# Larger expert blocks, rows scattered by slot and a combined last stage in a one-core decoder layer

## The chip, the core and the metric

The kernel runs on one core of one Trainium2 chip. The metric is the device time of one execution in microseconds; 5482.36 is the median of three runs of the kernel before (5481.67 to 5484.12). A core has a matrix engine (TensorE, PE), a vector engine (VectorE, DVE), a scalar engine (ScalarE, ACT), a programmable engine (GpSimd, POOL) that also issues indirect transfers, and a queue engine (SyncE, SP) that issues plain transfers. All transfers run on 16 shared DMA engines.

## The reference

One decoder layer on 16 sequences of 224 tokens with 512 features, 3584 tokens in all. It is a quantised self-attention, a cross-attention over 750 context rows, and a third block of attention across the 16 sequences followed by a mixture of experts. Only the last part and the norm behind it are touched:

```python
h1 = hidden_states + proj
ln2 = _layer_norm(h1, ln2_weight, ln2_bias)
probs = jax.nn.softmax(x @ router_weight, axis=-1)
top_p, top_i = jax.lax.top_k(probs, 2)          # 2 of 8 experts, shares normalised
cap = int(np.ceil(N * K / E * 1.25))            # 1120 slots for each expert
dst = jnp.where(within < cap, sorted_exp * cap + within, T)   # slot of each (token, choice)
padded_tokens = jnp.zeros((T, H)).at[dst].set(x[order // K], mode='drop')
fc1 = jax.nn.gelu(jnp.einsum('ech,ehf->ecf', xt, moe_w1))     # 512 -> 1024
fc2 = jnp.einsum('ecf,efh->ech', fc1, moe_w2)                 # 1024 -> 512
moe_out = jnp.zeros((N, H)).at[padded_tid].add(fc2 * padded_probs[:, None])
return h1 + moe_out
# and outside: x = _layernorm(x + ffn(x))
```

## The kernel before

The program is a row of stages. A stage is a `phase` (its semaphores, cleared by GpSimd when it ends) with one block in which each engine has its own instruction stream; the next stage starts when all engines have ended. Tokens stand in 28 tiles of 128 rows (`TT`), tile g of partition p being token 28p + g in the later stages.

Early in the program stands the stage `qm` (from line 422). TensorE computes all q, k and v products from rows and weights that are already in SBUF, and VectorE takes their largest magnitude. SP, ScalarE and GpSimd have nothing to do in it.

The end of the program is this:

- Stage `rt` (line 1792): the normalised rows `h1` are multiplied by the router's weights on TensorE; beside it SP stores `h1` to the DRAM table `l2_d` and zeros to `tid_d`. The residual `base` (x plus h1) stays in SBUF to the end of the program.
- Stage `sl` (line 1881): VectorE takes the two best experts of each token and gives each choice its slot; then GpSimd scatters token numbers by slot into `tid_d` with 56 indirect DMAs of 128 numbers (line 1889).
- Stage `tid` (line 1977): the token numbers are loaded, made float, turned on TensorE and copied back as integers, so that a column of them serves one tile.
- Stage `mo` (line 1994): the experts. `E` = 8 experts, each with `BLOCKS` = 5 blocks of `BT` = 2 tiles of `TS` = 112 slots. `loop4` runs three times over two experts in a hardware loop and then two experts written out. For each block GpSimd gathers the rows of the next block by token number (line 2052). TensorE multiplies with everything split into a high and a rest part, so each product is three matmuls (`three`, lines 2082 to 2084): first weights as stationary operand and 224 transposed token columns moving (8 groups f, two of which share a PSUM bank, 96 matmuls a block); then it transposes the next block's rows (line 2073, one bank for each tile, 8 transposes); then the second product, with gelu columns stationary (112) and 512 weight columns moving, 24 matmuls a tile. ScalarE does the gelu and the rounding to the high part (lines 2160, 2165), VectorE the rest part (line 2201), and both split the next block's transposed rows (lines 2151, 2194). The weights of the next expert are split beside it. SP loads weights (lines 2024, 2025) and stores the block's result rows to `y_d` (line 2037).
- Stage `cb` (line 2228): for each of 28 tiles GpSimd copies the slot numbers (line 2238) and gathers the two expert rows of each token (line 2242, 56 indirect DMAs of 256 KB), and VectorE adds them with their shares to `base` (lines 2257, 2259). Four tiles may be under way.
- Stage `nf` (`normalised`, line 254): VectorE takes the statistics of all tiles, ScalarE a square root, VectorE the inverse deviations and then the scaling.
- Stage `out` (line 2261): one store of 7168 KB.

TensorE, VectorE and ScalarE take their instructions in order; a waiting instruction holds up everything behind it on its engine.

## Time and profile before

| | |
|---|---|
| median of three runs | 5482.36 us |
| profiled execution | 5477.36 us |
| its span | 5475.4 us |
| PE busy | 3870.9 us (71%) |
| DVE busy | 2829.8 us (52%) |
| ACT busy | 1760.5 us (32%) |
| POOL busy | 654.2 us (12%) |
| moved by DMA | 266.11 MB |

Busy times are of the whole span, in which stages with different limits follow each other. The profile gives for each instruction its start, its duration, its shape and what ended the engine's idle time before it. `<-issue` stands for time in which the engine waited for nothing that the profile shows. The durations of a matmul overlap with the next one's; the distance of their starts is the pace. PEclk is the granted clock, 1.00 for 2.4 GHz and 0.50 for 1.2 GHz.

### The profile page before, as it was taken

How to read it: one execution, taken by the hardware profiler on the slowest of the kernel's cores; microseconds unless marked ns; L12 is line 12 of the kernel's file. 1: busy time of each engine (PE TensorE's matmuls, PEld its weight loads, DVE VectorE, ACT ScalarE, POOL GpSimd, SP SyncE). 2: the span in 40 equal slices, each digit the busy share in tenths (PEclk: the TensorE clock that was granted, in tenths of full speed). 3: DMA queues.
4: the chain of work that ended last, by engine and by line, in shares of the span. 5: the costliest groups of instructions: out<-in, count | busy, mean ns of one | idle time of the engine just before them, and what ended most of it. 6: DMA issues, size and time to landing. Idle time of an engine off the chain costs nothing. (4 is left out here: it accounts for less than half of the span.)

```text
span 5475.4 us, 83861 instructions
## 1 busy us (share of the span) xinstructions
PE 3870.9 (71%) x30253; PEld 2713.8 (50%) x30283; DVE 2829.8 (52%) x4238; ACT 1760.5 (32%) x3704; POOL 654.2 (12%) x490
## 2 busy tenths in 40 slices
PE   0499411394169999999999954888835599999960
PEld 0234311262046656666666633656515487878850
DVE  6766888897524444444444436777772122223224
ACT  0105079783023333333333321444411122232210
POOL 0000000000002222222222220000001301000113
PEclk9999555556579999999999986999965799999985
DMA  3001422232121001001001011000001222212213
GB/s 119 0 0 44 116 77 82 79 94 72 59 65 35 23 27 40 23 23 44 23 23 44 8 61 28 0 0 0 0 0 54 89 68 67 70 65 72 68 53 129
DMA packets 156402, 266.11 MB, mean 49 GB/s; under 512 B 75824, under 2 KB 75824, under 8 KB 155264
## 3 DMA queue, kind: packets, MB, share of 16 engines
q1 hardware_dynamic: 143488, 229.39, 13.1%
q0 software_dynamic: 12672, 33.07, 2.1%
q8 instruction: 204, 3.34, 0.3%
q14 instruction: 38, 0.31, 0.0%
HBM read 165.11 MB, written 67.96 MB: 43 GB/s over the span
## 5 line engine op out<-in xcount | busy, mean ns | idle before, releaser
L1393 DVE TENSOR_REDUCE arena<-psum 112x4 f32<-112x1504 f32 x256 | 441.4, 1724 | 768.7 <-PE psum L1223 768.6
L1137 POOL TENSOR_TENSOR arena<-arena 125x896 f32<-125x896 f32 x192 | 401.8, 2092 | 1255.1 <-ACT arena L1366 1255.1
L1366 ACT ACTIVATE arena<-psum 125x1792 f32<-125x1792 f32 x192 | 320.1, 1667 | 400.5 <-PE psum L1236 400.5
L2082 PE MATMUL psum<-tokens_T_high,w_high 128*128 128x224 f32 x1280 | 358.1, 280 | 29.8 <-PE psum L2084 14.9
L543 PE MATMUL psum<-arena 64*112 64x224 bf16 x1024 | 127.3, 401 | 348.7 <-DVEq L652 261.4
L2083 PE MATMUL psum<-tokens_T_rest,w_high 128*128 128x224 f32 x1280 | 354.5, 277 | 0.0
L2084 PE MATMUL psum<-tokens_T_high,w_rest 128*128 128x224 f32 x1280 | 353.9, 276 | 0.0
L668 ACT ACTIVATE arena<-arena,scales 112x224 bf16<-112x224 int8 x512 | 286.0, 559 | 35.3 <-DVEq L653 35.2
L2201 DVE TENSOR_TENSOR gelu_T_rest<-arena,gelu_T_high 128x448 fp32r<-128x448 f32 x160 | 100.1, 625 | 369.7 <-ACT gelu_T_high L2165 369.7
L2160 ACT ACTIVATE arena<-psum 128x448 f32<-128x448 f32 x160 | 87.0, 544 | 633.9 <-PE psum L2084 633.8
L543 PEld LDWEIGHTS psum<-arena 64*112 64x112 bf16 x1024 | 81.8, 200 | 394.4 <-DVEq L652 283.8
L1223 PE MATMUL psum<-arena 32*112 32x376 f32 x2048 | 236.2, 531 | 53.7 <-ACT arena L1366 27.0
L2082 PEld LDWEIGHTS psum<-tokens_T_high,w_high 128*128 128x128 f32 x1280 | 248.9, 194 | 47.1 <-issue 47.1
L2082 PE MATMUL psum<-w_high,gelu_T_high 128*112 128x512 f32 x640 | 255.8, 400 | 12.4 <-PE psum L2073 12.0
L417 PE MATMUL psum<-arena 128*128 128x512 bf16 x1104 | 250.6, 383 | 13.8 <-DVEq L457 8.0
L2084 PE MATMUL psum<-w_high,gelu_T_rest 128*112 128x512 f32 x640 | 252.5, 395 | 0.0
L2083 PE MATMUL psum<-w_rest,gelu_T_high 128*112 128x512 f32 x640 | 252.2, 394 | 0.0
L2083 PEld LDWEIGHTS psum<-tokens_T_rest,w_high 128*128 128x128 f32 x1280 | 249.0, 195 | 0.0
L2084 PEld LDWEIGHTS psum<-tokens_T_high,w_rest 128*128 128x128 f32 x1280 | 248.9, 194 | 0.0
L2211 DVE COPY arena<-psum 112x512 f32<-112x512 f32 x80 | 55.3, 692 | 345.6 <-PE psum L2084 345.6
L1232 PE MATMUL psum<-arena 32*125 32x224 f32 x3072 | 203.4, 380 | 43.2 <-DVE arena L1393 42.8
L1232 PEld LDWEIGHTS psum<-arena 32*125 32x125 f32 x3072 | 134.7, 186 | 120.5 <-DVE arena L1393 84.3
(297 smaller groups left out, 8818.4 us busy)
## 6 DMA issues: line engine op xcount, KB each, us to landing
arena<-L_ffn_moe_w SPq DMA_DIRECT2D x16, 2048.0 KB, 12.2
arena<-arena SPq DMA_DIRECT2D x32, 896.0 KB, 6.1
arena<-ctx SPq DMA_DIRECT2D x16, 1500.0 KB
expert_rows<-arena SPq DMA_DIRECT2D x40, 448.0 KB, 3.1
arena<-x SPq DMA_DIRECT2D x2, 7168.0 KB, 22.5
arena<-x_after_attn SPq DMA_DIRECT2D x32, 448.0 KB, 15.3
dots_ints<-arena SPq DMA_DIRECT2D x16, 784.0 KB, 4.8
arena<-dots_ints SPq DMA_DIRECT2D x16, 784.0 KB, 5.5
```

The lines of the kernel that those rows point to most:

```text
L417: last = PE.matmul(psum[:, j, :], qkvw_q[:, k, bass.ts(oc, P)], hT[:, k, j * D:(j + 1) * D], start=(k == 0), stop=(k == KC - 1))
L543: last = PE.matmul(psum[0:HALF, 4 * (hg % 2) + j, half * NS:(half + 1) * NS], stage[at, u, h // 2, half * HALF:(half + 1) * HALF], stage[a ...
L668: last = S.activation(junk[:, hg % 2, j, :], d8[:, u, h, (j % 2) * NS:(j % 2 + 1) * NS], ACT.Exp, bias=col("lowest")[0:HALF], scale=col("m ...
L1137: G.tensor_tensor(pair2[:, t, :, :], prob[:, t, :, 0:NS], prob[:, t, :, NS:2 * NS], ALU.add).then_inc(paired, 1)
L1223: last = PE.matmul(psum[0:HALF, j, 0:HC], qT[rows, u, g, half * HALF:(half + 1) * HALF], kT[rows, u, g, c * HC:(c + 1) * HC], start=True, ...
L1232: PE.matmul(psum[0:MC, j, s * NS:(s + 1) * NS], kT[rows, u, g, keys], qT[rows, u, g, :], start=(s == 0), stop=False)
L1366: S.activation(prob[:, t, :, :], score_psum(MC, 2 * NS), ACT.Exp, scale=SCALE2).then_inc(exp_done, 1)
L1393: return V.tensor_reduce(rmx[:, i // 2, i % 2, :], score_psum(HALF, HC), axis=AX.X, op=ALU.max).then_inc(r_free, 1)
L2082: PE.matmul(to, wh(k), xh(k), start=(k == 0), stop=False)
L2083: PE.matmul(to, wh(k), xl(k), start=False, stop=False)
L2084: last = PE.matmul(to, wl(k), xh(k), start=False, stop=(k == n - 1))
L2201: V.tensor_tensor(gTl[:, 2 * j:2 * j + 2, :], gT[:, j % 2, :, :], gTh[:, 2 * j:2 * j + 2, :].bitcast(F32), ALU.subtract).then_inc(g_rest, 1)
```

## The change

- Experts: 3 blocks of 3 tiles instead of 5 blocks of 2; the tiles have 128 slots and the last one of an expert 96 (384, 384 and 352 slots). The first product has one PSUM bank for each group f, three banks in turn; the transposes have two banks for three tiles; the second product has three banks.
- Rows by slot: the scatter in `sl` writes whole rows of 2 KB into `xs_d`, a table of 8960 slots, instead of token numbers. The table is filled with zeros in the stage `qm`. The token numbers, the stage `tid` and the gathers by token go; SP loads the rows of a block with two plain DMAs and stores the results with two.
- `base` is stored to `base_d` in `rt`, in the place of `h1`, and is loaded again at the end.
- `cb`, `nf` and `out` become one stage with 7 chunks of 4 tiles. GpSimd gathers up to 8 tiles ahead straight from the slot table. VectorE adds, takes statistics and computes scales one chunk later; ScalarE takes the root and does the scaling; SP stores each chunk.

The diff, cut to its core; of the last part only the new lines are shown, since the old stages `cb`, `nf` and `out` go whole.

```diff
@@ -419,7 +423,19 @@
             return last
 
         NOC = 3 * IN1 // P
+        with ExitStack() as st, phase(nc, "qm", "mm", "fr", "z", "zd") as (mm_done, bank_free, zero, zeroed), nc.Block() as block:
+            zeros = sb("zeros", [P, D], F32, st)
+
+            @block.gpsimd
+            def _(pool):
+                G.memset(zeros[:, :], 0.0).then_inc(zero, 1)
+
+            @block.sync
+            def _(sp):
+                sp.wait_ge(zero, 1)
+                sp.dma_start(xs_d.rearrange("(p a) d -> p a d", p=P), zeros[:, :].unsqueeze(1).broadcast_to([P, SLOTS // P, D])).then_inc(zeroed, 16)
+                sp.wait_ge(zeroed, 16)
+
...
+        base_d = scratch("x_plus_h1_rows", (T, D))
...
-                    sp.dma_start(l2_d.rearrange("(p g) d -> p g d", p=P), h1[:, :, :]).then_inc(rows_out, 16)
-
-                    sp.wait_ge(zeroed, 1)
-                    sp.dma_start(tid_d.rearrange("(a n) b -> a (n b)", a=80), zero_ids[:, :]).then_inc(rows_out, 16)
-                    sp.wait_ge(rows_out, 32)
...
+                    sp.dma_start(base_d.rearrange("(p g) d -> p g d", p=P), base[:, :, :]).then_inc(rows_out, 16)
+                    sp.wait_ge(rows_out, 16)
...
-                            pool.indirect_dma_start(out=tid_d[:, :], out_offset=bass.IndirectOffsetOnAxis(ap=slot_w[:, g, k:k + 1], axis=0),
-                                                    in_=row_id[:, g:g + 1], in_offset=None, bounds_check=SLOTS - 1,
+                            pool.indirect_dma_start(out=xs_d[:, :], out_offset=bass.IndirectOffsetOnAxis(ap=slot_w[:, g, k:k + 1], axis=0),
+                                                    in_=h1[:, g, :], in_offset=None, bounds_check=SLOTS - 1,
                                                     oob_is_err=False).then_inc(tp, 16)
...
+        BT = 3
+        BLOCKS = 3
+        BR = BT * P
         NF = FF // P
-        assert BLOCKS * TS * BT == CAP
-
...
+                def tokens(e, q, b, u):
+
+                    sp.wait_ge(x_read, b + 1)
+                    fence(sp)
+                    whole, rest = rows_of(xs_d, e, q)
+                    sp.dma_start(xg[:, u, 0:BT - 1, :], whole).then_inc(g_in[u], 16)
+                    sp.dma_start(xg[0:tile_rows(q, BT - 1), u, BT - 1, :], rest).then_inc(g_in[u], 16)
+
...
+                    if more:
+                        tokens(e + 1 if q == BLOCKS - 1 else e, (q + 1) % BLOCKS, b + 1, 1 - u)
...
-                    sp.dma_start(y_d[bass.ts(b, BT * TS), :].rearrange("(t p) d -> p t d", p=TS), yr[:, u, :, :]).then_inc(stored[u], 16)
+                    whole, rest = rows_of(y_d, e, q)
+                    sp.dma_start(whole, yr[:, u, 0:BT - 1, :]).then_inc(stored[u], 16)
+                    sp.dma_start(rest, yr[0:tile_rows(q, BT - 1), u, BT - 1, :]).then_inc(stored[u], 16)
...
+                        pe.wait_ge(xT_rest, BT * b + t + 1)
+                        n = tile_rows(q, t)
                         for k in range(KC):
-                            last = PE.transpose(psum[:, t, k * TS:(k + 1) * TS], xg[:, u, t, k * P:(k + 1) * P], ident[0:TS, 0:TS])
+                            last = PE.transpose(psum[:, t % 2, k * P:k * P + n], xg[0:n, u, t, k * P:(k + 1) * P], ident[0:n, 0:n])
...
-                        last = three(psum[:, 2 + f // 2, (f % 2) * 256:(f % 2) * 256 + BT * TS], lambda k: w1h[:, k, cols], lambda k: w1l[:, k, cols],
-                                     lambda k: xTh[:, k, :], lambda k: xTl[:, k, :], KC, split_w1)
-                        if f % 2 == 1:
-                            last.then_inc(f_mm, 1)
-
-                    pe.wait_ge(f_mm, (b + 1) * (NF // 2))
+                        three(psum[:, 2 + f % 3, 0:n], lambda k: w1h[:, k, cols], lambda k: w1l[:, k, cols],
...
+                        pe.wait_ge(y_moved, b * BT + t)
+                        n = tile_rows(q, t)
...
-                        three(psum[0:TS, 6 + t, :], lambda f: gTh[:, f, rows], lambda f: gTl[:, f, rows],
+                        three(psum[0:n, 5 + t, :], lambda f: gTh[:, f, rows], lambda f: gTl[:, f, rows],
...
+                    for f in range(NF):
+                        act.wait_ge(f_mm, b * NF + f + 1)
+
+                        act.wait_ge(g_rest, b * NF + f + 1)
+                        S.activation(gT[:, f % 2, 0:n], psum[:, 2 + f % 3, 0:n], ACT.Gelu_apprx_tanh).then_inc(gelu_done, 1)
+
+                        if f == 0:
+                            act.wait_ge(g_used, b)
+                        act.wait_ge(gelu_done, b * NF + f + 1 + 3)
...
+                        V.tensor_copy(yr[0:n, u, t, :], psum[0:n, 5 + t, :]).then_inc(y_moved, 1)
...
+            with phase(nc, "cb", "us", "ch", "var", "std", "rdy", "nrm", "o", *[f"x{i}" for i in range(NCH)], *[f"g{i}" for i in range(AHEAD)]) as (
+                    used, chs, var_done, std_done, scale_ready, normed, rows_out, *ins), nc.Block() as block:
+                x_in, g_in = ins[:NCH], ins[NCH:]
+
+                def chunk(i):
+                    return slice(i * LG, (i + 1) * LG)
+
+                @block.sync
+                def _(sp):
+                    for i in range(NCH):
+                        sp.dma_start(xf[:, chunk(i), :], base_d.rearrange("(p g) d -> p g d", p=P)[:, chunk(i), :]).then_inc(x_in[i], 16)
+                    for i in range(NCH):
+                        sp.wait_ge(normed, i + 1)
+                        sp.dma_start(out_d.rearrange("(p g) d -> p g d", p=P)[:, chunk(i), :], xf[:, chunk(i), :]).then_inc(rows_out, 16)
+                    sp.wait_ge(rows_out, 16 * NCH)
 
                 @block.gpsimd
                 def _(pool):
+                    for i in range(TT):
+                        if i >= AHEAD:
+                            pool.wait_ge(used, (i - AHEAD) // LG + 1)
+                        for k in range(2):
+                            pool.indirect_dma_start(out=yg[:, i % AHEAD, k, :], out_offset=None, in_=y_d[:, :],
+                                                    in_offset=bass.IndirectOffsetOnAxis(ap=slot_r[:, i, k:k + 1], axis=0),
+                                                    bounds_check=SLOTS - 1, oob_is_err=False).then_inc(g_in[i % AHEAD], 16)
 
                 @block.vector
                 def _(dve):
+                    ch = Chain(dve, chs)
+
+                    def scales(i):
+                        at = fstat[:, chunk(i), :]
+                        dve.wait_ge(std_done, i + 1)
+                        ch.link(V.reciprocal(at[:, :, 2], at[:, :, 1]))
+                        ch.link(V.tensor_tensor(at[:, :, 3], at[:, :, 2], at[:, :, 2], ALU.mult))
+                        ch.link(V.tensor_tensor(at[:, :, 3], at[:, :, 3], at[:, :, 4], ALU.mult))
+                        ch.link(V.scalar_tensor_tensor(at[:, :, 2], at[:, :, 3], 1.5, at[:, :, 2], ALU.add, ALU.mult))
+                        V.scalar_tensor_tensor(at[:, :, 5], at[:, :, 6], -1.0, at[:, :, 2], ALU.mult, ALU.mult).then_inc(scale_ready, 1)
+
+                    for i in range(NCH):
+                        tiles = range(i * LG, (i + 1) * LG)
+                        dve.wait_ge(x_in[i], 16)
+                        for t in tiles:
+                            dve.wait_ge(g_in[t % AHEAD], 32 * (t // AHEAD + 1))
+                            done = V.scalar_tensor_tensor(xf[:, t, :], yg[:, t % AHEAD, 0, :], share[:, t, 0:1], xf[:, t, :], ALU.mult, ALU.add)
+                        ch.link(done)
+                        for t in tiles:
+                            done = V.scalar_tensor_tensor(xf[:, t, :], yg[:, t % AHEAD, 1, :], share[:, t, 1:2], xf[:, t, :], ALU.mult, ALU.add)
+                        ch.link(done)
+                        dve.sem_inc(used, 1)
+                        for t in tiles:
+                            done = V.bn_stats(pieces[:, t, :], xf[:, t, :])
+                        ch.link(done)
+                        for t in tiles:
+                            done = V.bn_aggr(fstat[:, t, 6:8], pieces[:, t, :])
+                        ch.link(done)
+                        V.tensor_scalar(fstat[:, chunk(i), 4], fstat[:, chunk(i), 7], col("eps"), -0.5, ALU.add, ALU.mult).then_inc(var_done, 1)
+                        if i >= 1:
+                            scales(i - 1)
+                    dve.wait_ge(var_done, NCH)
+                    scales(NCH - 1)
+
+                @block.scalar
+                def _(act):
+                    def normalise(i):
+                        act.wait_ge(scale_ready, i + 1)
+                        for t in range(i * LG, (i + 1) * LG):
+                            done = S.activation(xf[:, t, :], xf[:, t, :], ACT.Identity, bias=fstat[:, t, 5:6], scale=fstat[:, t, 2:3])
+                        done.then_inc(normed, 1)
+                    for i in range(NCH):
+                        act.wait_ge(var_done, i + 1)
+                        S.activation(fstat[:, chunk(i), 1], fstat[:, chunk(i), 7], ACT.Sqrt, bias=col("eps"), scale=1.0).then_inc(std_done, 1)
+                        if i >= 1:
+                            normalise(i - 1)
+                    normalise(NCH - 1)
         L3.close()
```

## Rows read from the trace of the kernel before

**Rows 1.** Stage windows: span:us, busy (count) of PE, PEld, DVE, ACT, POOL; PEclk, DMA share, GB/s.

```profile
225.70:381.00 155.30, 150.63 (x672) 64.12 (x672) 97.18 (x48) 0.00 (x0) 0.00 (x0) 1.00 0.00 0
...
4292.80:5301.50 1008.70, 940.03 (x6080) 802.53 (x6080) 271.39 (x384) 281.69 (x470) 91.31 (x120) 0.98 0.22 70
...
5301.50:5409.50 108.00, 0.00 (x0) 0.00 (x0) 42.21 (x56) 0.00 (x0) 63.32 (x84) 0.51 0.49 140
...
5409.50:5475.40 65.90, 0.00 (x0) 0.00 (x0) 36.18 (x98) 1.63 (x2) 0.00 (x0) 0.50 0.26 112
```

**Rows 2.** Timeline, TensorE, one expert block: start us, us, engine, line, operation.

```profile
4735.60 0.37 PE L2082 MATMUL psum<-tokens_T_high,w_high 128*128 128x224 f32 x1 [0.38 <-PE psum L2084]
...
4735.81 0.27 PE L2083 MATMUL psum<-tokens_T_rest,w_high 128*128 128x224 f32 x1
...
4746.31 0.27 PE L2084 MATMUL psum<-tokens_T_high,w_rest 128*128 128x224 f32 x1
...
4746.96 0.98 PE L2073 MATMUL psum<-ident,arena 112*128 112x112 f32 x8 [0.38 <-PE psum L2084]
...
4748.23 0.48 PE L2082 MATMUL psum<-w_high,gelu_T_high 128*112 128x512 f32 x1 [0.28 <-PE psum L2073]
...
4748.55 0.39 PE L2083 MATMUL psum<-w_rest,gelu_T_high 128*112 128x512 f32 x1
...
4759.22 0.39 PE L2084 MATMUL psum<-w_high,gelu_T_rest 128*112 128x512 f32 x1
...
4759.99 0.37 PE L2082 MATMUL psum<-tokens_T_high,w_high 128*128 128x224 f32 x1 [0.38 <-PE psum L2084]
```

**Rows 3.** Timeline, ScalarE and VectorE at the end of that block's first product.

```profile
4746.61 0.54 ACT L2160 ACTIVATE arena<-psum 128x448 f32<-128x448 f32 x1 [1.53 <-PE psum L2084]
...
4747.19 0.57 ACT L2165 CAST gelu_T_high<-arena 128x448 fp32r<-128x448 f32 x1
...
4747.66 0.96 ACT L2151 CAST tokens_T_high<-psum 128x448 fp32r<-128x448 f32 x2
...
4748.33 1.15 DVE L2194 TENSOR_TENSOR tokens_T_rest<-psum,tokens_T_high 128x448 fp32r<-128x448 f32 x2
```

**Rows 4.** Timeline, TensorE, return of the expert loop.

```profile
4813.08 0.52 PE L2082 MATMUL psum<-tokens_T_high,w_high 128*128 128x224 f32 x1 [4.55 <-issue]
```

**Rows 5.** Timeline, POOL and SP, scatter of slots and the stage behind it.

```profile
4212.40 0.98 POOL L1889 DMA_INDIRECT token_of_slot<-arena  x1 [0.30 <-issue]
...
4281.33 0.97 POOL L1889 DMA_INDIRECT token_of_slot<-arena  x1 [0.31 <-issue]
...
4289.32 0.33 SPq L1980 DMA_DIRECT2D arena<-token_of_slot  x1
...
4292.78 0.40 SPq L2024 DMA_DIRECT2D arena<-L_ffn_moe_w  x1
```

**Rows 6.** Timeline, POOL, a gather beside VectorE's splitting of the first weights.

```profile
4308.08 1.94 POOL L2052 DMA_INDIRECT arena<-tokens_for_experts,arena  x1 [0.30 <-issue]
```

**Rows 7.** Timeline, combination and last norm.

```profile
5308.44 1.06 POOL L2242 DMA_INDIRECT arena<-expert_rows,arena  x1 [0.93 <-POOL arena L2238]
...
5309.80 1.00 POOL L2242 DMA_INDIRECT arena<-expert_rows,arena  x1 [0.30 <-issue]
...
5313.74 0.75 DVE L2257 SCALAR_TENSOR_TENSOR arena<-arena 128x512 f32 x1 [12.30 <-DMA arena<-expert_rows,arena]
...
5409.81 2.47 DVE L218 BATCH_NORM_STATS2 ln_parts<-arena 128x6 f32 x4 [1.43 <-PEq L46]
...
5436.86 0.21 DVE L234 TENSOR_TENSOR arena<-arena 128x28 f32<-128x28 f32 x1
```

**Rows 8.** DMA issues: line, engine, count, KB each, us to landing.

```profile
expert_rows<-arena SPq DMA_DIRECT2D x40, 448.0 KB, 3.1
...
out<-arena SPq DMA_DIRECT2D x1, 7168.0 KB, 18.3
```

252 lines of the change are left out of this document (92 added, 160 removed).

## The prediction

> **What bounds the kernel now.** I read the stage windows first, then the timeline inside a stage, then the page's list of DMA issues. The profiled execution took 5477.36 us around a span of 5475.4. The stages that the change touches run one after the other, so each is priced alone. In the expert stage TensorE is busy 940 of 1008.7 us at full clock while DMA stands at 0.22: TensorE's instruction stream sets that stage. The combination of 108 us and the last norm with store of 66 us have no TensorE work; in the first POOL is busiest (63 us) with DVE and DMA near half, in the second DVE works and then everybody waits for one store [rows 1]. The stage in which the zeroing is put has 155.3 us with TensorE busy and no DMA at all [rows 1].
>
> One expert block (two tiles of 112) is read off the timeline [rows 2]. The first product's matmuls (224 columns) start at 4735.81 and 4746.31, 94 steps apart: 0.1117 us each. The second product's (512 columns) start at 4748.55 and 4759.22, 46 steps: 0.2320 us each. The slope is (0.2320 - 0.1117) / 288 = 0.4177 ns a column, and what is left at no columns is 18 ns. So a step with 384 columns is estimated at 0.1785 us, with 352 at 0.1652. Beside the steps a block pays 0.21 us for its first step, 0.65 from the last first-product matmul to the transposes, 1.27 for eight transposes and the change to the second product, 0.32 for that product's first step and 0.77 to the next block. The block lasts 24.39 us.
>
> **The change part by part: the expert blocks.** Before, an expert is 5 blocks, 122.0 us. After, it is 3, with 384, 384 and 352 rows. First product: 0.21 + 94 x 0.1785 + 0.72 (the last matmul is some 0.07 longer) = 17.71 us; in the third block 0.21 + 94 x 0.1652 + 0.70 = 16.44. Second product, three tiles of 24 steps: 0.32 + 70 x 0.2320 + 0.77 = 17.33.
>
> The transposes between them get a new wait. Three tiles share two PSUM banks, so the third tile's transposes wait until ScalarE and then VectorE have read the first tile's bank. ScalarE comes to it only after the last gelu and its copy; before, the same chain ran beside the second product and nobody waited [rows 3]. From the end of the last first-product matmul (4746.58): the gelu starts at +0.03 and its copy at +0.61, the copies of x at +1.08, the subtraction on VectorE at +1.75 [rows 3]. With gelu and copy narrower by 64 columns (about 0.05 us each) and the x tile wider by 64 (about 0.06 on each engine, estimates from 0.57 us for 448 columns), the first bank is free near +2.4. Four transposes (0.6) and the switch (0.3) put the second product at +3.3, which is 2.9 after the transposes' start. Twelve transposes with no wait would take 1.7, so the wait costs about 1.2 us a block. It could be nothing, or up to 3 us if the hand-overs are slow. The waits behind it in TensorE's queue are the whole second product; everything else on ScalarE and VectorE has slack (busy 282 and 271 of 1008.7 us [rows 1]).
>
> An expert is then 2 x (17.71 + 2.91 + 17.33) + 16.44 + 2.85 + 17.33 = 112.5 us. Over eight experts, leaving out the transposes after the last block: before 975.6 - 1.3 = 974.3, after 900.2 - 2.9 = 897.3: **-77 us**. What the stage holds beside its blocks, the loading of the first weights and two stalls at the loop's end of 4.55 us each, one of them shown [rows 4], stays. The weight tile of the second product becomes 128 wide, not 112; the first product already has 128 and the same 18 ns left over, so I take nothing; at most 16 columns more at 0.4177 ns, 1728 times, +11.5 us.
>
> Token rows now come by plain loads on SP (768 KB, an estimate of some 4 us from 448 KB in 3.1 [rows 8]) rather than by indirect gathers. They are issued ahead of the weights, as soon as the block before has been stored, 17 us before they are needed: hidden. In the first block they stand ahead of the first weights and the third tile takes one more round: +2.
>
> **Zeroing.** 18.35 MB on SP in a stage that nothing else on SP uses. At the rate of the last store (7.34 MB in 18.3 us [rows 8], 401 GB/s) it lasts 46 us, at that of the gathers (140 GB/s at a share of 0.49, so some 286 at full share [rows 1]) 64. The 155.3 us of that stage hide it: 0. Without that cover it would cost the 46 to 64.
>
> **The scatter.** 56 indirect DMAs stay; each moves 256 KB instead of 512 bytes. POOL issues one every 1.276 us (4212.40 to 4281.33, 54 steps [rows 5]), 71.5 us in all. 256 KB in 1.276 us is 205 GB/s, under the 286 that gathers of such rows could reach, so POOL remains the limit. The last one's landing is now waited for with 256 KB behind it; a gather of that size lands 3.9 us after its issue (5309.80 to its first use at 5313.74 [rows 7]), the small writes of now sooner, so the term lies between 0 and +3.9 and I take +1.4. No row shows a scatter of 2 KB rows: at the store's rate it would be hidden, at half the gathers' rate it would take 102 us, +31. I take the first, since the rows have the same size as those of the gathers.
>
> The stage that turned slot numbers round goes: 4289.32 to 4292.78 [rows 5], **-3.5 us**. Storing the residual instead of the normalised rows is the same 7.34 MB in the same place, beside the router's TensorE work: 0.
>
> **The end as one stage.** Before, from the first gather at 5308.44 to the end is 167.0 us [rows 7]. After, POOL issues 56 gathers without copies and, in the first eight tiles, without waits. The nearest paces are 1.28 [rows 5] and 1.36 [rows 7]; I take 1.33. The last starts 73.2 us after the first and lands 3.9 later: 77.1. A chunk needs on VectorE eight scaled sums (0.75 each, some 0.7 back to back), four bn_stats (2.47) and some ten short steps (0.21 us and a link each) [rows 7]: 10.6 us, the same as POOL's 10.6. So both go in step, and after the last landing VectorE needs 7.2 us to the variances and 2.5 for two rounds of scales. Then ScalarE scales four tiles twice (0.57 for 448 columns [rows 3], so some 2.2 a chunk, half of it already done) and a 1 MB store lands in 4.4 (between 3.1 for 448 KB and 18.3 for 7168 KB [rows 8]). That makes 95 us with what lies behind the last landing. In its first half the stage also loads 7.3 MB, and the whole stage moves 29.4 MB: by DMA time 14.7 MB / 286 + 14.7 MB / 401 = 88 us, close enough that I add 3. 98 against 167.0, and the first gather comes 1.1 us earlier: **-70 us**. Ends: -75 if nothing collides, -45 if POOL is held up as below.
>
> **Sum.** -77 + 2 + 1.4 - 3.5 - 70 = -147. 5477.36 - 147 = 5330.3. The median of the runs shown, 5482.36, lies 5.0 above the profiled execution, so the forecast is 5335.3, taken as **5335**.
>
> **Rivals.** First, VectorE holds POOL up in the last stage. One row speaks for it: an indirect DMA that ran beside VectorE's subtraction of two SBUF operands took 1.94 us [rows 6], others 0.97 to 1.06. VectorE now does such operations for 6 of every 10.6 us beside the gathers. If each gather under one took 1.94, the pace would be 1.33 + 0.57 x 0.96 = 1.88, the gathers 105 us and the gain 30 less: 5365. Against it: the gathers of now run beside the same operation at 1.36 and less. The Trainium skill, SBUF - State Buffer, section Who interferes with whom, says that such an operation contends only with GpSimd's reads while descriptor generation needs writes; by that rule the gathers keep their pace and the sum stands, and the 1.94 is something else. Chance 0.13.
>
> Second, the scatter is limited by DMA, +31 as worked out: 5366. Chance 0.08.
>
> Third, the new wait for a PSUM bank does not show, because ScalarE and VectorE are faster than their chain looks: 23 x 1.2 = 28 us less, 5307. Chance 0.05. Its opposite, 3 us a wait, gives 5335 + 41 = 5376. Chance 0.05.
>
> Fourth, the other side: the change doesn't hide the zeroing. Its source is one 2 KB row read 70 times in each partition, and no row shows such a transfer. If it ran on few of the 16 engines, say one (401 / 16 = 25 GB/s), it would take 732 us, 577 beyond its stage: 5912. It makes the kernel slower from where it needs over 155 + 147 = 302 us, 61 GB/s. Against it: 128 partitions as the outermost count, as in every fast store of the page. Chance 0.03.
>
> **How the numbers follow.** The forecast holds 0.66. The range takes in the absent wait below and the two held-up cases and most of the bounds above: 5303 to 5376. About 0.2% (11 us) is what a measurement of this kernel can tell from no change. All cases but the fourth are faster by far more: faster 0.96, same 0.01, slower 0.03.
>
> **What would show it.** In the trace after: first-product steps of 0.178 us and second-product steps of 0.232; an idle of about 1.2 us in the middle of each block's transposes, released by VectorE; block periods near 37.9 and 36.6; scatter steps of 1.28 us; the zeroing landed within 70 us; the last stage near 100 us, its gathers 1.33 apart and VectorE busy over 70 us. Gathers or scatters above 1.5 us, a first-product step far from 0.178, or idle TensorE at each expert's start would break the sum.

## The result and the profile after

| | before | after |
|---|---|---|
| median | 5483.24 us (5481.67 to 5485.00, 4 runs) | 5400.20 us (5393.20 to 5408.76, 4 runs) |
| profiled execution | 5477.36 us | 5393.20 us |

The ratio is 0.9851, with a 95% interval from 0.9839 to 0.9864. The kernel is 83 us faster. The forecast was 5335 us with a range from 5303 to 5376, so the direction held, and the time lies 24 us above the top of the range.

The page of the kernel after, its first lines (busy time of each engine):

```profile
span 5391.4 us, 79574 instructions
...
PE 3799.4 (70%) x28522; PEld 2650.6 (49%) x28522; DVE 2819.3 (52%) x4252; ACT 1799.0 (33%) x3794; POOL 559.7 (10%) x341
```

The stages of the kernel after, the same view as [rows 1]: the stage with the zeroing, the third attention, the experts, the end:

```profile
226.10:382.40 156.30, 151.50 (x672) 64.31 (x672) 97.19 (x49) 0.00 (x0) 0.05 (x1) 1.00 0.31 117
3262.80:4121.90 859.10, 581.94 (x3968) 402.24 (x3968) 576.01 (x1089) 272.54 (x1054) 0.42 (x2) 0.87 0.04 13
4302.70:5281.60 978.90, 859.24 (x4320) 741.06 (x4320) 273.74 (x400) 296.89 (x526) 0.00 (x0) 0.98 0.21 72
5281.60:5391.40 109.80, 0.00 (x0) 0.00 (x0) 66.04 (x154) 23.80 (x36) 59.42 (x56) 0.50 0.76 268
```

The zeroing now fills part of a stage that had no DMA, and costs it 1 us. The experts have the same mean granted clock as before (0.98), but TensorE is busy only 859 of 979 us, where [rows 1] had 940 of 1009. The end has DMA at 0.76.

To place the difference, the span is cut at five marks that both kernels have: the load of the residual for the third attention, the store of the residual (before: of the normalised rows), the first DMA of the experts, the first gather of the end, and the last instruction. Every piece is a difference of two starts in the timeline, in us:

| kernel | to the third attention | third attention | router and scatter | experts | end |
|---|---|---|---|---|---|
| before | 3267.5 | 841.9 | 183.4 | 1015.7 | 167.0 |
| after | 3262.8 | 859.2 | 180.7 | 980.1 | 108.6 |
| predicted change | 0 | 0 | -2.1 | -76.1 | -69.0 |
| measured change | -4.7 | +17.3 | -2.7 | -35.6 | -58.3 |

The measured changes add up to -84.0, the difference of the two spans. The predicted ones, cut at the same marks (the 1.1 us by which the first gather was to come earlier count to the experts), add up to -147.2. The missing 63 us are 40.5 in the experts, 17.3 in a stage that the prediction did not look at, and 10.7 in the end, less the 4.7 and 0.6 us by which the first piece and the router came out lower than forecast. The first piece holds the zeroing, and otherwise code that nothing touches; in the profiled executions of all runs below but the one with four zeroings it lies between 3261.8 and 3276.9 us, so its 4.7 us mean nothing. The other pieces differ less between runs whose code is the same in them: 980.1 to 985.7 us for the experts as in the kernel after (seven runs), 107.8 to 108.9 for its end (six runs), 859.2 to 866.1 for its third attention (seven runs), and 840.7 to 842.0 for the third attention as before (five runs).

**An expert block.** TensorE's timeline, which answers to [rows 2] (start us, us, engine, line, operation, and in brackets the idle time before it with what ended it):

```profile
4363.60 0.44 PE L2066 MATMUL psum<-tokens_T_high,w_high 128*128 128x384 f32 x1 [0.42 <-PE psum L2068]
...
4380.93 1.09 PE L2057 MATMUL psum<-ident,arena 128*128 128x128 f32 x8 [0.40 <-PE psum L2068]
4382.98 0.55 PE L2057 MATMUL psum<-ident,arena 96*128 96x96 f32 x4 [0.97 <-DVE tokens_T_rest L2179]
4383.83 0.47 PE L2066 MATMUL psum<-w_high,gelu_T_high 128*128 128x512 f32 x1 [0.30 <-PE psum L2057]
...
4390.41 0.50 PE L2066 MATMUL psum<-w_high,gelu_T_high 128*128 128x512 f32 x1 [0.86 <-DVE arena L2197]
...
4396.93 0.50 PE L2066 MATMUL psum<-w_high,gelu_T_high 128*128 128x512 f32 x1 [0.78 <-DVE arena L2197]
...
4403.06 0.42 PE L2066 MATMUL psum<-tokens_T_high,w_high 128*128 128x352 f32 x1 [0.38 <-PE psum L2068]
```

The first product takes 17.33 us (4363.60 to 4380.93; predicted 17.71), the transposes with the switch to the second product 2.90 (predicted 2.91), in which TensorE idles 0.97 us before the third tile's transposes. But the second product takes 19.23 us (predicted 17.33): each of its later tiles stands 0.86 and 0.78 us idle for VectorE's L2197, the copy-out of the tile just finished. The list of TensorE's waits between 4345 and 5280 us (engine, line, who was waited for: us in total, times, longest):

```profile
PE psum L2066 <- DVE arena L2197: 39.2, 48, 0.9
PE psum L2057 <- DVE tokens_T_rest L2179: 21.5, 22, 1.0
```

**The third attention.** The windows of two tiles before, then of three after (columns as in [rows 1]), each followed by rows of the eight score matmuls, which begin a tile's work on TensorE:

```profile
3405.20:3428.10 22.90, 19.72 (x140) 13.78 (x140) 16.18 (x28) 10.28 (x38) 0.00 (x0) 1.00 0.01 1
3428.10:3451.20 23.10, 19.75 (x140) 13.80 (x140) 16.19 (x28) 8.99 (x37) 0.00 (x0) 1.00 0.00 0
...
3405.22 3.67 PE L1643 MATMUL psum<-arena_attn 128*128 128x512 f32 x8 [1.86 <-DVE arena L1767]
```

```profile
3401.20:3425.90 24.70, 21.42 (x140) 14.37 (x140) 16.21 (x28) 10.29 (x38) 0.00 (x0) 0.93 0.01 2
3425.90:3449.20 23.30, 19.75 (x140) 13.78 (x140) 16.20 (x28) 9.00 (x37) 0.00 (x0) 1.00 0.00 0
3449.20:3473.90 24.70, 21.42 (x140) 14.35 (x140) 16.20 (x28) 10.29 (x38) 0.00 (x0) 0.93 0.00 0
...
3401.23 5.37 PE L1653 MATMUL psum<-arena_attn 128*128 128x512 f32 x8 [1.94 <-DVE arena_attn L1777]
...
3425.93 3.70 PE L1653 MATMUL psum<-arena_attn 128*128 128x512 f32 x8 [1.85 <-DVE arena_attn L1777]
```

Here every second tile has a granted clock of 0.93 and takes 24.7 us instead of 23. In it the eight score matmuls take 5.37 us instead of 3.67. They run so in 8 of the 28 tiles, in none before, and 8 x 1.7 = 14 of the 17.3 us are that. What changed on the way to them is one row: the operations on VectorE's queue at the residual addition, before (L1765) and after (L1775):

```profile
L1765 DVEq FUSED_REGOPS  x26: 93/96/99, 3403.4 to 3979.3; - x26
```

```profile
L1775 DVEq FUSED_REGOPS  x26: 93/93/93, 3399.3 to 3990.2; - x26
L1775 DVEq ALU_OP  x26: 40/40/40, 3399.5 to 3990.3; - x26
```

The addition reads `base` and writes `h1`. Before, `base` was the first buffer of its arena, at offset 0. Now both lie at the upper end of one arena, and the address of a tile of `base` takes one more register operation, 40 ns; with what lies around it the addition starts 0.08 us later. (`h1` lies at the upper end of an arena in both kernels.) TensorE's idle time before the score matmuls, which wait for VectorE's next addition (L1777), went from 49.0 us in 27 tiles to 51.0, in the mean from 1.81 to 1.89 us each. In both kernels it is not the same in every tile: it goes 1.86, 1.77, 1.86, 1.77 before and 1.94, 1.85, 1.94, 1.85 after. All 8 slow tiles stand behind one of the 14 gaps of 1.94.

**The end.** Timeline rows of SP, POOL, VectorE and ScalarE, which answer to [rows 7]:

```profile
5281.63 4.15 SPq L2226 DMA_DIRECT2D arena<-x_plus_h_rows  x7
...
5282.77 1.06 POOL L2238 DMA_INDIRECT arena<-expert_rows,arena  x1 [987.89 <-issue]
5284.14 1.01 POOL L2238 DMA_INDIRECT arena<-expert_rows,arena  x1 [0.30 <-issue]
...
5293.50 0.75 DVE L2260 SCALAR_TENSOR_TENSOR arena<-arena 128x512 f32<-128x512 f32 x1 [17.83 <-DMA arena<-expert_rows,arena]
...
5299.39 0.75 DVE L2260 SCALAR_TENSOR_TENSOR arena<-arena 128x512 f32<-128x512 f32 x1 [5.13 <-DMA arena<-expert_rows,arena]
...
5313.79 1.00 POOL L2238 DMA_INDIRECT arena<-expert_rows,arena  x1 [10.17 <-DVEq L2265]
```

```profile
5379.39 5.75 ACT L2283 ACTIVATE arena<-arena 128x512 f32<-128x512 f32 x8 [0.59 <-DVE arena L2253]
```

The gathers are issued 1.31 us apart, as expected. But the seven loads of the residual went out 1.1 us ahead of them, and the first tile is complete 10.7 us after its gather, not 5.3 as in [rows 7]. The first chunk is late, its buffers are released late, and POOL stands for 10.17 us. At the end ScalarE scales eight tiles in one go (5.75 us), since the scales of a chunk are computed behind the variances of the next; the prediction had taken half of one chunk as done by then. The transfers, answering to [rows 8] (KB each, us from issue to landing; the loads take 17.4 us each, the stores of the same size 5.4):

```profile
rows_by_slot<-arena SPq DMA_DIRECT2D x1, 17920.0 KB, 49.3
...
arena<-x_plus_h_rows SPq DMA_DIRECT2D x7, 1024.0 KB, 17.4
out<-arena SPq DMA_DIRECT2D x7, 1024.0 KB, 5.4
...
rows_by_slot<-arena_attn,arena POOLq DMA_INDIRECT x56, 2.6
```

### The profile page after: what moved, and what is told of

Same layout as the page of the kernel before. It is cut to its first block and busy times, and to the rows that moved or that the text cites. A ratio compares the mean times of both kernels' runs of the same rounds, so it can differ in the third digit from the quotient of the medians.

```text
span 5391.4 us, 79574 instructions
## 1 busy us (share of the span) xinstructions
PE 3799.4 (70%) x28522; PEld 2650.6 (49%) x28522; DVE 2819.3 (52%) x4252; ACT 1799.0 (33%) x3794; POOL 559.7 (10%) x341
## 3 DMA queue, kind: packets, MB, share of 16 engines
q0 software_dynamic: 8960, 26.58, 1.4%
## 5 line engine op out<-in xcount | busy, mean ns | idle before, releaser
L2066 PE MATMUL psum<-tokens_T_high,w_high 128*128 128x384 f32 (+1 forms) x768 | 259.5, 338 | 19.9 <-PE psum L2068 9.2
L2066 PE MATMUL psum<-w_high,gelu_T_high 128*128 128x512 f32 (+1 forms) x576 | 231.9, 403 | 46.6 <-DVE arena L2197 39.2
L2187 DVE TENSOR_TENSOR gelu_T_rest<-arena,gelu_T_high 128x384 fp32r<-128x384 f32 (+1 forms) x192 | 104.6, 547 | 294.0 <-ACT gelu_T_high L2150 294.0
L2067 PE MATMUL psum<-tokens_T_rest,w_high 128*128 128x384 f32 (+1 forms) x768 | 256.9, 334 | 0.0
L2068 PE MATMUL psum<-tokens_T_high,w_rest 128*128 128x384 f32 (+1 forms) x768 | 256.8, 334 | 0.0
L2197 DVE COPY arena<-psum 128x512 f32<-128x512 f32 (+1 forms) x72 | 49.7, 690 | 363.6 <-PE psum L2068 363.6
L2067 PE MATMUL psum<-w_rest,gelu_T_high 128*128 128x512 f32 (+1 forms) x576 | 225.2, 391 | 0.0
L2068 PE MATMUL psum<-w_high,gelu_T_rest 128*128 128x512 f32 (+1 forms) x576 | 225.0, 391 | 0.0
L1260 PE MATMUL psum<-arena 125*32 125x224 f32 x3072 | 187.3, 362 | 5.4 <-ACT arena L1382 5.4
L421 PEld LDWEIGHTS psum<-arena 128*128 x1120 | 107.4, 99 | 158.3 <-issue 38.1
L1160 PE MATMUL psum<-ctx_T_high,Wk_high 128*128 128x376 f32 x512 | 183.2, 358 | 0.0
## 6 DMA issues: line engine op xcount, KB each, us to landing
rows_by_slot<-arena SPq DMA_DIRECT2D x1, 17920.0 KB, 49.3
```

The costliest lines, as they stand in the source:

```text
L421: last = PE.matmul(psum[:, j, :], qkvw_q[:, k, bass.ts(oc, P)], hT[:, k, j * D:(j + 1) * D], start=(k == 0), stop=(k == KC - 1))
L1260: last = PE.matmul(psum[DH2 * j:DH2 * (j + 1), 6 + g % 2, 0:NS], vR[:, u, mt, h * DH2:(h + 1) * DH2], prob[:, t, j, s * NS:(s + 1) * NS], ...
L2066: PE.matmul(to, wh(k), xh(k), start=(k == 0), stop=False)
L2067: PE.matmul(to, wh(k), xl(k), start=False, stop=False)
L2068: last = PE.matmul(to, wl(k), xh(k), start=False, stop=(k == n - 1))
```

## The experiments

Times are medians of four runs (five in one case), ratios are to runs of the kernel before on the same chip; a difference to the kernel after compares medians that were not taken together, so it is read beside the length of the piece in the traces. The theory: three causes take the gain. First, the wait at L2092 makes each tile of the second product wait for the copy-out of the tile before it. Secondly, one more register operation lengthens a gap of TensorE in the third attention, and the granted clock falls. Thirdly, the loads of the residual collide with the first gathers. The rivals are that VectorE sets the pace of the experts, that the clock's fall is chance, and that the end is bound by its transfers as a whole.

### The wait set back by a block (e1_y_wait)

```diff
-                        pe.wait_ge(y_moved, b * BT + t)
+                        pe.wait_ge(y_moved, b * BT + t + 1)
-                    sp.wait_ge(y_moved, b * BT + BT)
+                    sp.wait_ge(y_moved, b * BT + 2 * BT)
...
                 def first():
+                    dve.sem_inc(y_moved, BT)
```

> The changed kernel, with the wait before the tiles of the second product set back by one block: tile t waits for the copy-out of tile t of the block before, which read the same bank, and no longer for tile t - 1 of its own block. Theory: in the changed kernel TensorE idles 0.78 us before each second and third tile, 48 times (39 us), and about 0.2 us of drain and start lies around each; all of it goes, 46 to 50 us below the changed kernel, so 5350 to 5354 us. Rival: VectorE, which also has the copies, the splits and the weights to do, is the engine that sets the pace there, and the idle time only moves to the first product's start: 0 to 10 us.

Measured: 5354.10 us, ratio 0.9769 (0.9753 to 0.9785), 46 us under the kernel after; the experts 935.3 us instead of 980.1. The waits of TensorE between 4345 and 5240 us:

```profile
PE psum L2057 <- DVE tokens_T_rest L2179: 22.5, 23, 1.0
PE psum L2057 <- PE psum L2068: 10.0, 23, 0.6
```

The wait for L2197 is gone and nothing took its place. The theory is confirmed and the rival refuted. The experts are now 80.4 us shorter than before the change, 4 more than predicted.

A block that starts at 4367.30 lasts 37.2 us, against 39.5 with the wait: 2.2 us a block, 54 in 24 blocks. The stage gained less, 44.8, and the windows of two blocks show why:

```profile
4367.30:4404.50 37.20, 35.14 (x180) 31.24 (x180) 8.36 (x15) 9.60 (x19) 0.00 (x0) 1.00 0.13 41
...
4478.40:4517.10 38.70, 36.69 (x180) 32.34 (x180) 8.30 (x15) 9.60 (x19) 0.00 (x0) 0.96 0.12 40
```

Both are middle blocks of an expert, yet the second lasts 1.5 us longer at a granted clock of 0.96; its first eight second-product steps are 0.43 us apart instead of 0.23. They come right behind the third tile's idle 0.97 us. Six blocks are like that, about 9 us. The kernel after itself has no such block, but this is chance in part: of the six other profiled runs with the same expert code as it, one has four such blocks, one three, one two and three have one, each time behind that wait.

### Three banks for the transposes (e4_three_banks)

```diff
-  PE.transpose(psum[:, t % 2, k * P:k * P + n], ...
+  PE.transpose(psum[:, (0, 1, 7)[t], k * P:k * P + n], ...
-  pe.wait_ge(y_moved, b * BT + t)
+  pe.wait_ge(y_moved, b * BT + (BT + max(t - 1, 0)))
-  three(psum[0:n, 5 + t, :], ...
+  three(psum[0:n, 5 + t % 2, :], ...
```

The counts of `xT_rest` and `y_moved` start at 3, and the readers use the same banks.

> The changed kernel, with the PSUM banks dealt out otherwise: the three tiles of transposes have three banks (0, 1, 7) and no longer wait for each other, and the second product's tiles use banks 5 and 6 in turn, tile t waiting for the copy-out of the tile two before it. So both waits inside a block go: the one priced in the run with the wait set back (46 us), and the third tile's 0.96 us of idle TensorE in 23 blocks. Theory: the second wait lies wholly on TensorE's path, 20 to 25 us more, so 65 to 75 us under the changed kernel, 5325 to 5335 us. Rival: the second product needs what ScalarE and VectorE make of the last gelu anyway, so TensorE only waits a little later for the rest part of gelu: 46 to 55 us under it, 5345 to 5354 us.

Measured: 5321.70 us, ratio 0.9704 (0.9688 to 0.9720), 78.5 under the kernel after, more than the theory's 65 to 75; the experts 896.6 us. The twelve transposes now run without a stop:

```profile
4424.59 1.53 PE L2057 MATMUL psum<-ident,arena 128*128 128x128 f32 x12 [0.55 <-PE psum L2068]
4426.41 0.47 PE L2066 MATMUL psum<-w_high,gelu_T_high 128*128 128x512 f32 x1 [0.30 <-PE psum L2057]
```

```profile
4372.30:4408.30 36.00, 34.91 (x180) 31.27 (x180) 8.30 (x15) 9.50 (x19) 0.00 (x0) 1.00 0.13 43
...
4479.90:4515.90 36.00, 34.91 (x180) 31.27 (x180) 8.29 (x15) 9.50 (x19) 0.00 (x0) 1.00 0.13 43
```

Middle blocks last 36.0 us instead of 37.2. Dealing only two banks in turn to the second product brings no wait back. So the third tile's wait costs 1.22 us, the prediction's "about 1.2", 28 us in 23 blocks. The 38.7 that the stage gained over the run before are these 28, the 9 of the clock, which is 1.00 here, and 1 in the first block. The rival, that TensorE then waits for the rest part of gelu, is refuted.

### One register operation less, in two ways (e2_base_own, e12_base_low)

```diff
+        base = own("x_plus_h1", [P, TT, D], F32, L3a)
-        open_arena("arena_3_attn", SBUF - ARENA_3, L3a)
-        base = sb("x_plus_h1", [P, TT, D], F32, L3a, "high")
+        open_arena("arena_3_attn", SBUF - ARENA_3 - TT * D * 4, L3a)
```

> The changed kernel, with the residual x_plus_h1 in an SBUF tensor of its own instead of at the upper end of the arena that also holds h1. Nothing else is changed; the address of a tile of it then takes one register operation less on VectorE (40 ns, 26 times before the residual addition of the third attention). Theory: that operation lengthens TensorE's gap before the score matmuls by 0.08 to 0.09 us, and with the longer gap the granted clock falls in 8 of 28 tiles; both go, 15 to 18 us below the changed kernel, the stage back from 859 to about 842 us. Rival: the clock's fall has nothing to do with that operation; then only the gaps go, 28 times 0.08 to 0.13 us, 2 to 4 us.

Measured: 5382.70 us, ratio 0.9823 (0.9807 to 0.9840), 17.5 under the kernel after. The third attention lasts 840.7 us. The second way keeps one arena and changes a word:

```diff
-        base = sb("x_plus_h1", [P, TT, D], F32, L3a, "high")
+        base = sb("x_plus_h1", [P, TT, D], F32, L3a)
```

> The changed kernel, with x_plus_h1 at the lower end of the same arena, at offset 0, instead of at its upper end. The instructions of every engine are the same but for one register operation less on VectorE ahead of each residual addition (L1775), as an address with no constant part needs none. Theory: that operation of 40 ns alone is the cause of the half-clock tiles in the third attention: 15 to 18 us below the changed kernel, no score matmuls at 5.37 us for eight, as with the tensor of its own. Rival: sharing one SBUF tensor with h1 is the cause (the own tensor removed both): 0 to 3 us below.

Measured: 5382.01 us, ratio 0.9823 (0.9807 to 0.9840), 18.2 under; the third attention 840.9 us. The score matmuls and the queue operations at L1775:

```profile
L1653 PE MATMUL psum<-arena_attn x224: 592/592/697, 3379.3 to 4004.2; 128*128 128x512 f32 x112
...
  DVE arena_attn L1777: 49.0, 27
```

```profile
L1775 DVEq FUSED_REGOPS  x26: 93/96/99, 3400.6 to 3976.4; - x26
```

No score matmul takes over 0.70 us (1.06 in the kernel after), the idle time is back at 49.0, the operation of 40 ns is gone. In the second way the engines' instructions in this piece differ in nothing else but seven such operations less at L272, in the norm outside the loop over the tiles. So the operation in front of 26 additions cost 18 us. Sharing a tensor is not the cause; where `base` lies in it is. `h1` keeps its place at the upper end and needs no such operation at this line, so an offset other than 0 alone does not explain it; what the rule of the addresses is, no run here tells.

### The kernel before with a longer gap (e9_before_gap, e10_before_gap1)

The added line stands three times in the first and once in the second.

```diff
                     y = h1[:, bass.ts(g, 1), :].rearrange("p a d -> p (a d)")
+                    fence(dve) 
                     ch.link(V.tensor_tensor(y, psum[:, 6, :], x, ALU.add))
```

> The kernel before, with three semaphore increments more on VectorE ahead of the residual addition of the third attention (behind the wait for TensorE's projection), 0.1 to 0.2 us in each of 28 tiles, on the path to the next score matmuls. Theory: a longer gap on TensorE there makes the granted clock fall in some of the tiles, so it costs more than its own time: 10 to 25 us over the kernel before. Rival: it costs its own time, 3 to 6 us, at a granted clock of 1.00.

> The kernel before, with one semaphore increment more on VectorE ahead of the residual addition of the third attention. With three of them TensorE's gap grew by 0.28 us a tile, the score matmuls of some tiles ran at half clock, and the kernel took 24 us more. If the clock depends on that gap at a point between 1.81 us (always full clock) and 1.89 us (the changed kernel, 8 of 28 tiles at half clock), one of them, 0.09 us, should already give 10 to 20 us. Rival: the cost grows in proportion to the delay: 24 / 3 = 8 us or less.

Measured: with three, 5504.21 us, ratio 1.0044 (1.0027 to 1.0061); with one, 5504.86 us, ratio 1.0038 (1.0024 to 1.0053). Both are some 24 us slower than the kernel before. The idle time before the score matmuls is 2.10 us a tile with three and 1.91 with one. Windows with one, of a tile with fallen clock and a full one:

```profile
3409.30:3434.00 24.70, 21.42 (x140) 14.38 (x140) 16.16 (x28) 10.28 (x38) 0.00 (x0) 0.93 0.01 2
...
3458.90:3481.90 23.00, 19.72 (x140) 13.77 (x140) 16.18 (x28) 10.28 (x38) 0.00 (x0) 1.00 0.00 0
```

With one, 13 tiles have eight score matmuls of 5.37 to 5.40 us: 13 x 1.7 + 27 x 0.10 = 25 us. With three, ten tiles have them and the gaps add 8 us: again 25. The cost is not in proportion to the delay. That refutes both rivals: the delay alone would be 3 us with one. The cost with one lies above the 10 to 20 us that were expected. How many tiles fall cannot be read from the gap: the seven profiled runs with a mean gap of 1.89 us have 8 to 12 of them, the one with 1.91 has 13, the one with 2.10 has 10, and the five with 1.81 have none. Nor does a longer gap always do it: with a mean of 1.89 the clock fell only behind the gaps of 1.94 and not behind each, but with one increment it fell behind seven gaps of 1.87 us and not behind eight of 1.95. What picks the tiles no run here tells.

### The loads in the end (e3_loads_staged, e13_ahead16, e11_one_load)

```diff
-                    for i in range(NCH):
-                        sp.dma_start(xf[:, chunk(i), :], ...).then_inc(x_in[i], 16)
+                    load(0)
+                    load(1)
+                    sp.wait_ge(used, 1)
+                    load(2)
                     for i in range(NCH):
+                        if i + 3 < NCH:
+                            sp.wait_ge(used, i + 2)
+                            load(i + 3)
                         sp.wait_ge(normed, i + 1)
```

> The changed kernel, with the seven loads of x_plus_h1 in the last stage spread out: chunks 0 and 1 at once, each later one when the chunk two before it has been added up. Theory: the seven loads at once (7 MB) share the DMA engines with the first gathers, so that the first tile is ready 10 us after its first gather was issued and GpSimd later waits 10 us for free buffers; spread out, the first tile is ready after about 4 us and the stage takes 8 to 12 us less. Rival: the same bytes have to move anyway and the DMA engines bound the stage, so they only collide later: 0 to 3 us.

Measured: 5395.74 us, ratio 0.9846 (0.9830 to 0.9863), which the whole time can't tell from the kernel after. The stage can: 102.6 us instead of 108.6. POOL no longer waits, and its last gather is issued 75.2 us after the first, not 85.1. The gain of 6.0 us lies between the theory (8 to 12) and the rival (0 to 3). The first sum comes 7.8 us after the first gather.

```diff
-            AHEAD = 8
+            AHEAD = 16
```

> The changed kernel, with buffers for 16 tiles of gathered rows instead of 8 in the last stage; the loads of x_plus_h1 still go out all at once. GpSimd then doesn't stop for 10 us behind the first chunk. Theory: the stop was what the late first chunk cost, so the stage loses 6 us or more, as with the staged loads. Rival: the gathers are only issued earlier and their data come no sooner, since the DMA engines are the limit: 0 to 3 us.

Measured: 5396.75 us, ratio 0.9856 (0.9839 to 0.9872), no difference in the whole; the stage 103.7 us, 4.9 less. The last gather is issued 75.0 us after the first, but the first tile is still complete only after 10.6, and VectorE, now behind, works the chunks off at 9.7 us each. It lies between the two expectations.

```diff
-                    for i in range(NCH):
-                        sp.dma_start(xf[:, chunk(i), :], ...
+                    for i in range(1):
+                        sp.dma_start(xb[:, :, :], ...
...
-   done = V.scalar_tensor_tensor(xf[:, t, :], yg[...], share[:, t, 0:1], xf[:, t, :], ...)
+   done = V.scalar_tensor_tensor(xf[:, t, :], yg[...], share[:, t, 0:1], xb[:, t % LG, :], ...)
```

> The changed kernel, with one load of 1 MB of x_plus_h1 in the last stage instead of seven; every chunk adds to the same rows, so that 6.3 MB of transfers are left out (and the output is that of other residuals). Theory: beside the first gathers the loads hold up the DMA engines, and later they take a share that the gathers lack: the stage (108.6 us from the first gather to the end) falls to 93 to 98 us, 11 to 16 us below the changed kernel, and 5 to 9 us below the staged loads. Rival: the rest of the stage goes by GpSimd's pace and VectorE's chain; then no gain over the staged loads, about 6 us below the changed kernel.

Measured: 5391.61 us, ratio 0.9841 (0.9824 to 0.9857); the stage 98.9 us. VectorE's first sum comes 5.7 us after the first gather, the next ones without a long stop:

```profile
5299.25 0.75 DVE L2262 SCALAR_TENSOR_TENSOR arena<-arena 128x512 f32<-128x512 f32 x1 [12.80 <-DMA arena<-expert_rows,arena]
...
5301.34 0.82 DVE L2262 SCALAR_TENSOR_TENSOR arena<-arena 128x512 f32<-128x512 f32 x1 [1.34 <-DMA arena<-expert_rows,arena]
```

So the six loads that are left out cost the stage 9.7 us, a little less than the 11 to 16 expected and more than the rival's 6: about 6 because all are issued ahead of the gathers, and 4 as traffic that spreading them in this way does not remove.

### Four times the zeroing (e7_zero_four)

```diff
+                for i in range(4):
+                    sp.dma_start(xs_d..., zeros...).then_inc(zeroed, 16)
+                    sp.wait_ge(zeroed, 16 * (i + 1))
```

> The changed kernel, with the table of rows by slot filled with zeros four times over, one after the other, in the same stage. One takes 49.3 us, four 197, the stage lasts 156. Theory (hidden while it is shorter than the stage): the stage becomes as long as the four transfers, 40 to 46 us more than the changed kernel. Rival: the transfers already slow the stage beside them, by 1 us each: then some 3 us come on top.

Measured: 5444.33 us, ratio 0.9930 (0.9913 to 0.9946), 44 over the kernel after. SP's row, and TensorE's wait behind the stage:

```profile
226.30 148.25 SPq L437 DMA_DIRECT2D rows_by_slot<-arena  x4
```

```profile
PE psum L421 <- DVEq L474: 49.3, 1, 49.3
```

The fourth starts at 226.30 + 148.25 = 374.6 us and lasts as long as the others, 49.4; the stage would have ended near 382. TensorE starts behind the stage at 429.5 us, 42 later than in the kernel after (387.8). Its last matmul of the stage ends at 380.2 us, against 379.6 with one zeroing, so the rival, 1 us for each transfer, does not show. One zeroing is hidden, and the cover ends where the stage does.

### Everything together (e5_all, e14_best)

The first version joins the three banks, the tensor of its own and the staged loads, and computes the scales of a chunk ahead of the second sums of the next one, so that ScalarE scales it before it takes the next root. The second puts `base` low, has buffers for 16 tiles, and computes the scales behind the release of the buffers:

```diff
                         ch.link(done)
                         dve.sem_inc(used, 1)
+                        if i >= 1:
+                            scales(i - 1)
```

> Everything together on the changed kernel: the banks dealt out as in the run with three banks for the transposes, x_plus_h1 in a tensor of its own, its loads at the end spread out, and in the last stage the scales of a chunk computed in the middle of the next chunk instead of behind it, so that ScalarE scales four tiles after the last variance and not eight (2.9 us). If the causes add up: 5400 - 46 - 20 - 17 - 6 - 3 = 5308, between 5300 and 5316 us. Rival: they hide each other, the staged loads and the own tensor above all; then it is above 5316.

> The version with everything together, changed in three places: x_plus_h1 at the lower end of its arena instead of in a tensor of its own, buffers for 16 tiles of gathered rows in the last stage instead of 8, and the scales of a chunk computed right behind the release of the gather buffers and not ahead of it. Theory: in the version with everything the last stage lasted 104.9 us, as GpSimd stopped twice for buffers (6.5 us); here it doesn't stop and ScalarE has four tiles to scale at the end: 98 to 101 us, the kernel 4 to 7 us under that version, 5288 to 5292 us. Rival: the DMA engines limit the stage, and issuing gathers earlier brings nothing: 5293 us or more.

Measured: 5295.70 us, ratio 0.9663 (0.9647 to 0.9679), and 5293.78 us, ratio 0.9662 (0.9646 to 0.9678). The first lies below its range (5300 to 5316), since its sum has 66 us for the two waits in the experts and the run with three banks measured 78.5; the rival, that the causes hide each other, is refuted for the experts and the third attention. In the first version's trace the third attention takes 842.0 us (17.2 less than after), the experts 896.3 (83.8 less) and the end 104.9 (3.7 less, where the sum had 9). Both are 3.4% faster than the kernel before, where the change alone gave 1.5%. The second was expected at 5288 to 5292 us; between the two no difference can be told: three executions of the second lie at 5289 to 5294 us and its profiled one at 5310, with stalls in the end for which the profile names no cause, so its last stage is not read here, and whether 16 buffers help this version stays open. In the first version POOL waited for buffers 6.5 us in all, since the scales stand ahead of the release; the 2.9 us of scaling saved at the end did not show in the stage.

## Why the prediction was wrong, point by point

**The second product (40 us).** The step that failed is "Second product, three tiles of 24 steps: 0.32 + 70 x 0.2320 + 0.77". It takes the change from tile to tile for a plain step, without a wait. The diff shows `pe.wait_ge(y_moved, b * BT + t)`: in the kernel before the count rose once a block and the wait was for `b`, the block before; now it rises once a tile, and tile t waits for copy t of its own block. The prediction asked who waits at the new bank of the transposes and passed over this wait. It gave VectorE slack from its busy time, 271 of 1008.7 us, but TensorE needs one copy at one moment, and a busy time says nothing of that. VectorE's copy takes 0.69 us, TensorE idles 0.82 for it and a change of tile costs about 1.1 in all: 44.8 us in the stage by the first experiment, net of the clock that fell in six blocks. The Trainium skill, Perfetto Trace Analysis, section Matmuls, says that independent groups of matmuls should rotate through PSUM banks so that the copy-out of one overlaps the next. The three banks here are such a rotation, and the trace shows that the semaphore's count undid it.

**The third tile's wait.** Right: 0.97 us idle and 1.22 us a block against "about 1.2 us". Not foreseen was that the idle time can lower the clock behind it, which it did in six blocks of the first experiment.

**The steps.** 0.1736 us for 384 columns ((17.33 - 0.27 - 0.74) / 94) against 0.1785, and 0.227 for 512 against 0.2320. With the wait mended a block of 384 lasts 37.22 us against 37.95, one of 352 36.51 against 36.62. The stage then measured -80.4 against -76.1, and would be 9 lower still without the fallen clock: the steps are where that comes from.

**The third attention (17 us).** Here a term was missing. The change moves `base` into the arena of `h1`, and the prediction has nothing for this stage, so it stands in the sum with 0 us and no reason. The code of the stage was unchanged but for addresses. The longer gaps themselves are 2 us of the 17.3; about 14 are the clock behind them.

**The end (11 us).** Right was the pace of the gathers (1.31 against 1.33), and near was what remains without the loads: 98.9 us with one, 95 predicted with none. Of these 4 us, 2.5 are ScalarE, which at the end scales eight tiles in 5.75 us where the sum had 3.3. The term that was mis-sized is "close enough that I add 3" for the transfers: six of the seven loads cost 9.7. The sum of DMA time said that they fit into the stage, but not when they fall: all seven in front of the first gather.

**Router and scatter.** Right: -2.7 against -2.1. The scatter's pace is 1.28 us with 256 KB each, landing after 2.6.

**The zeroing.** Right: 49.3 us, between the bounds of 46 and 64, and hidden; the stage is 1 us longer.

**The rivals.** That VectorE holds POOL up did not happen: the gathers of the end keep 1.31 us. They last 1.06 us on average. The 25 that run beside none of VectorE's sums take 1.00 (one 1.06); of the 31 beside one, 18 take 1.00 to 1.02 and 13 take 1.13 to 1.41, none the 1.94 of the rival. The rule cited for this from the Trainium skill (SBUF - State Buffer, Who interferes with whom) agrees with the pace; why 13 gathers are longer no run here shows. The scatter was not limited by DMA, the bank wait was neither absent nor 3 us, and the zeroing used all engines: a DMA share of 0.31 over the stage's 156.3 us is 48.5 us of all 16, and it lasted 49.3. None of the rivals was the wait inside the second product, so the range had no place for it.

## What to carry to other kernels

When a semaphore's count is made finer, work out for each waiter which event it now waits for, tile by tile, and compare that with the buffer it wants to use; a rotation of banks is worth nothing if the count names the tile just before. When buffers move between arenas, compare the instructions of every stage that uses them: here one operation of 40 ns in front of an addition that TensorE waits for cost 18 us, and putting the buffer at offset 0 gave them back. In a stage that starts with gathers, issue only the loads that the first chunk needs.

## What the runs showed of the hardware that was not expected

- TensorE's granted clock fell in the third attention in 8 to 13 of 28 tiles where the gap before the score matmuls was 1.89 to 2.10 us in the mean, and in none where it was 1.81. The single gaps behind which it fell are 1.87 to 2.14 us long; it never fell behind those of 1.86 or less. Where it fell, the eight matmuls behind the gap ran at 1.2 instead of 2.4 GHz and took 5.37 us instead of 3.67. In the experts it also fell behind an idle time of 0.96 to 1.02 us: in six of 24 blocks of the run with the wait set back, in none to four of those with the expert code of the kernel after, and, apart from the return of the hardware loop, nowhere in the three runs without that idle time.
- A buffer indexed at run time cost VectorE's queue one register operation of 40 ns less at the lower end of its arena than at the upper end, in 26 of 26 additions.
- A fill of 18.35 MB from one 2 KB row in each partition landed in 49.3 us, 372 GB/s, and four of them one after the other kept that pace beside a busy TensorE.
